# Norm work in single-tile pieces, statistics of four images in one group, and late sends of two images in a four-layer MetaFormer with mixtures of experts

## The reference

```python
x = x + mixer(layernorm(x))          # L0 fractal, L1 involution, L2 KAN spline, L3 attention
t = tokens(x)                        # 8192 x 128
t = t + experts(layernorm(t))        # for each token the chosen experts alone count
# layer    experts E   choices K   hidden F
#   0         8           1          512     relu, capacity 1.25, nan_to_num at the end
#   1         8           2          512     gelu, softmax over the two
#   2         8           2          256     gelu, softmax over all, top two
#   3        16           2          256     silu(x w1) * (x w2) w3, top two renormalised
def layernorm(v):
    return (v - mean(v, -1)) / sqrt(var(v, -1) + 1e-6)   # 1e-5 ahead of the experts
```

## Time and profile before

| | |
|---|---|
| runs | 2220.95, 2220.1, 2215.83 us (median 2220.1) |
| the profiled execution | 2214.52 us, its span 2212.8 us |
| mean granted TensorE clock | 0.909 |
| busy in the span | PE 1774.9, DVE 1546.8, ACT 1197.6, POOL 953.9 us |
| indirect DMAs on GpSimd | 488 returns, 448 sends |

### The profile page before, as it was taken

One profiled execution on the slowest core, in us unless ns is written; L12 is line 12 of the kernel. 1 busy time (PEld: TensorE's weight loads), 2 busy tenths in 40 slices (PEclk: granted clock), 3 DMA queues, 4 the chain that ended last, 5 costly groups with the idle time before them and its releaser, 6 DMA issues. The chain is left out here.

```text
span 2212.8 us, 44512 instructions
## 1 busy us (share of the span) xinstructions
PE 1774.9 (80%) x10980; PEld 1391.5 (63%) x10981; DVE 1546.8 (70%) x4832; ACT 1197.6 (54%) x2708; POOL 953.9 (43%) x953
## 2 busy tenths in 40 slices
PE   2588666898588888999895866797859999888986
PEld 2234566898344344899884434686657777687986
DVE  6998887689677777655776667557765777754564
ACT  4455776799233233777674333565664444454653
POOL 0000234444113443665442377777510446466664
PEclk9999766999699999999997877889969999989998
DMA  3002002232200010233341112235330002023373
GB/s 79 0 0 76 15 27 60 60 99 74 86 11 29 29 58 27 65 98 101 105 117 39 53 52 79 79 107 171 116 117 21 27 33 59 31 69 97 106 216 102
DMA packets 183598, 154.35 MB, mean 70 GB/s; under 512 B 40294, under 2 KB 162822, under 8 KB 183362
## 3 DMA queue, kind: packets, MB, share of 16 engines
q1 hardware_dynamic: 153410, 92.37, 15.6%
q0 software_dynamic: 29952, 59.26, 7.9%
HBM read 85.33 MB, written 68.79 MB: 70 GB/s over the span
## 5 line engine op out<-in xcount | busy, mean ns | idle before, releaser
L1706 POOL DMA_INDIRECT returned<-rows_second_choice x488 | 506.9, 1039 | 370.7 <-DVE rows_second_choice L1631 151.7
L1492 PE MATMUL psum<-rows_first_choice 128*128 128x128 f32 x2816 | 387.3, 282 | 28.7 <-DVE rows_first_choice L1612 27.8
L1263 POOL DMA_INDIRECT dispatched<-rows_first_choice,slot x192 | 191.5, 998 | 487.1 <-DVE rows_second_choice L1159 434.9
L1492 PEld LDWEIGHTS psum<-rows_first_choice 128*128 128x128 f32 x2816 | 352.0, 196 | 38.0 <-DVE rows_first_choice L1612 36.7
L1502 PE MATMUL psum<-expert_weights,rows_first_choice 128*128 x2240 | 325.4, 284 | 28.3 <-DVE rows_second_choice L1628 11.8
L1502 PEld LDWEIGHTS psum<-expert_weights,rows_first_choice 128*128 128x128 f32 x2240 | 284.4, 195 | 41.7 <-issue 37.4
L1562 ACT ACTIVATE rows_first_choice<-psum,bias_columns 128x128 f32<-128x128 f32 x832 | 238.7, 374 | 106.9 <-PE psum L1492 105.3
L1263 POOL DMA_INDIRECT dispatched<-rows_second_choice,slot x192 | 187.6, 977 | 58.5 <-issue 58.2
L1263 POOL DMA_INDIRECT dispatched<-rows_first_choice,expert_weights x64 | 62.0, 969 | 267.2 <-DVE rows_first_choice L1157 249.9
L1545 ACT ACTIVATE rows_first_choice<-expert_weights 128x512 f32 x216 | 137.3, 636 | 40.2 <-issue 40.1
L1484 PE MATMUL psum<-identity,rows_second_choice 128*128 128x128 f32 x488 | 138.4, 285 | 16.2 <-DMA rows_second_choice<-dispatched 16.1
(11 more groups left out here) (416 smaller groups left out, 3814.3 us busy)
## 6 DMA issues: line engine op xcount, KB each, us to landing
rows_second_choice<-dispatched SPq DMA_DIRECT2D x488, 65.0 KB
rows_second_choice<-returned SPq DMA_DIRECT2D x10, 1024.0 KB, 5.5
returned<-rows_second_choice POOLq DMA_INDIRECT x488
expert_weights<-in_L_ffn_w SPq DMA_DIRECT2D x3, 2048.0 KB, 8.6
expert_weights<-returned SPq DMA_DIRECT2D x6, 1024.0 KB, 5.4
channel_major<-returned SPq DMA_DIRECT2D x6, 1024.0 KB, 5.7
residual<-in_x SPq DMA_DIRECT2D x8, 512.0 KB, 7.3
rows_second_choice<-returned SPq DMA_DIRECT2D x8, 512.0 KB, 4.0
```

Source lines behind the costliest of these rows:

```text
L1263: pool.indirect_dma_start(out=self.k.dispatched, out_offset=bass.IndirectOffsetOnAxis(ap=self.slot[:, b % 2, c, t:t + 1], axis=0), in_=sel ...
L1492: ins = pe.matmul(k.ps[:, self.PSH + u % 2, j * P:(j + 1) * P], self.wc[:, u % 2, j * P:(j + 1) * P], self.xt[:, u % 2, :], start=True, st ...
L1706: pool.indirect_dma_start(out=k.returned[0:N * self.K, :], out_offset=bass.IndirectOffsetOnAxis(ap=self.rt[:, u, C:C + 1].bitcast(I32), ax ...
```

## The change

- **Opening**: `norm.vector` stands ahead of the wait for GpSimd and of the four casts.
- **NormStage**: statistics in groups of four, two and two images in place of four pairs. A table STEPS for each layer, with one small piece a tile: an add of half an image (128x512), four bn_stats, one Newton round, two or three norms. Images 6 and 7 are both done after the last tile in every layer.
- **GpSimd**: in layer 0's tail it adds six images to x (128x1024). In layer 1's tail it adds the two choices of six images into each other in the room they were loaded to, and VectorE adds that to x in halves. In layer 2's tail VectorE adds both choices in halves.
- **LastStage**: later loads and stores, adds in halves at other steps.
- **Last layer**: five first images (64 first tiles in place of 48). Images 6 and 7 are sent between the returns: image 6 one block every second tile from tile 0, image 7 one every fourth tile from tile 16. In layer 1 image 7's blocks go every second tile.
- VectorE reads the next tile's expert number ahead of the norm piece in layers 1 and 2.

```diff
@@ opening
             ins.then_inc(s_set.h, 1)
-            dve.wait_ge(s_set.h, 7)
+            norm.vector(dve)
             dve.wait_ge(s_made.h, 8)
             dve.tensor_copy(k.rank[:], int_rank[:])
...
-            norm.vector(dve)
@@ class NormStage
-    PAIRS = B // 2
+    GROUPS = ((0, 1, 2, 3), (4, 5), (6, 7))
-    LOAD_AFTER = [None, (55, 56, 60, 64, 68, 71), (87, 91, 99, 107, 115, 123), (88, 92, 104, 110, 118, 124)]
-    PAIR_AT = [None, (46, 54, 62), (78, 94, 110), (92, 108, 124)]
-    SIXTH_AT = [None, None, 126, None]
-    TAKE = [None, (0, 2), (0, 3), (0, 3)]
-    FINISH = [None, 4, 6, 6]
-    INVERT = [None, 6, 9, 9]
+    STEPS = [
+        None,
+        dict(load=(55, 56, 60, 64, 68, 71), fold=(43, 44, 48, 52, 56, 60), collect=(50, 52, 54, 58, 63, 67),
+             finish=(60, 69), root=(61, 70), offset=(62, 71), norm=(63, 65, 67, 69, 72, 74),
+             turn=(65, 67, 69, 71, 74, 76), keep=(66, 68, 70, 72, 75, 77)),
+        dict(load=(87, 88, 89, 93, 103, 119), fold=(75, 77, 79, 83, 91, 107), add=(80, 84, 88, 92, 105, 112),
+             collect=(82, 86, 90, 94, 107, 114), finish=(96, 116), root=(97, 117), offset=(101, 121),
+             norm=(102, 104, 106, 108, 122, 124), turn=(105, 107, 109, 111, 125, 127),
...
+        dict(load=(87, 88, 89, 97, 103, 119), add=(78, 84, 90, 96, 116, 122), collect=(82, 88, 94, 100, 120, 126),
+             finish=(102, 128), root=(103, 129), offset=(107, 133), norm=(108, 110, 112, 114, 134, 136),
...
+    def gpsimd_step(self, pool, t):
+
+        for b in range(B - 2):
+            if self.adds < 4 and t == self.steps["fold"][b]:
+                pool.wait_ge(self.s_back[b].h, self.s_back[b].base + 16)
+                xs, room = self.image(b), self.room(b)
+                if self.choices == 1:
+                    pool.tensor_tensor(xs, xs, room, ALU.add).then_inc(self.s["rows_added"].h, 1)
+                else:
+                    pool.tensor_tensor(room[:, :, 0:C], room[:, :, 0:C], room[:, :, C:2 * C],
+                                       ALU.add).then_inc(self.s["choices_folded"].h, 1)
...
+    def add_folded(self, dve, b, h):
+
+        dve.wait_ge(*self.when("choices_folded", b + 1))
+        xs = self.image(b)[:, self.half(h)]
+        dve.tensor_tensor(xs, xs, self.room(b)[:, self.half(h), 0:C], ALU.add).then_inc(self.s["rows_added"].h, 1)
...
+    def add_half(self, dve, b, c, h):
+
         if c == 0:
             dve.wait_ge(self.s_back[b].h, self.s_back[b].base + 16)
...
-    LEFT = 24
+    LEFT = 12
@@ class LastStage
-    LOAD_AFTER = (96, 98, 100, 102, 112, 128)
+    LOAD_AFTER = (112, 114, 116, 118, 120, 128)
     COMPLETE = 128
-    ADD_AT = (88, 91, 94, 97, 104, 120, 136)
-    STORE_AFTER = (108, 111, 114, 117, 124, 140)
+    ADD_AT = (104, 108, 112, 116, 120, 126, 138)
+    STORE_AFTER = (122, 126, 130, 134, 138, 142)
@@ Router, TAILS
-FIRST_IMAGES = 4
+FIRST_IMAGES = (4, 4, 4, 5)
+HELD_FROM = (7, 7, 7, 6)
...
-        for b in range(B - 1):
+        for b in range(HELD_FROM[self.layer]):
             self.send(pool, b)
...
-    dict(pe=(0, 4, 5, 8), dve=(0, 2, 6, 9, 10), act=(2, 4, 7), send=9),
-    dict(pe=(0, 6, 8, 12), dve=(0, 3, 9, 13, 14), act=(3, 6, 10), send=12),
-    dict(pe=(0, 6, 8, 12), dve=(0, 3, 9, 13, 14), act=(3, 6, 10), send=12),
...
+    dict(pe=(0, 4, 5, 8), dve=(0, 2, 6, 9, 10), act=(2, 4, 7), send={7: (9, 2)}),
+    dict(pe=(0, 6, 8, 12), dve=(0, 3, 9, 13, 14), act=(3, 6, 10), send={7: (12, 1)}),
+    dict(pe=(0, 6, 8, 12), dve=(0, 3, 9, 13, 14), act=(3, 6, 10), send={6: (0, 2), 7: (16, 4)}),
@@ class Experts
             if at >= self.table_end:
+                if self.vector_copies and t + 2 < self.T:
+                    ahead.append(self.expert_of(dve, t + 2))
                 self.following.vector_step(dve, t)
...
+            for b, (start, every) in held.items():
+                if t == start:
+                    route.slots_known(pool, b)
+                    pool.wait_ge(*route.sent(b - 1, b % 2))
+                n = t - start
+                if 0 <= n < TPB * every and n % every == 0:
+                    route.send_tile(pool, b, n // every)
...
+            if t >= self.table_end:
+                self.following.gpsimd_step(pool, t)
```

More of the change, by code:

```diff
@@ L459, in gpsimd, with image, half @@
             self.involution.make_gather(pool)
-    def add(self, dve, b, c):
-        k = self.k
+    def image(self, b):
+        return self.k.x[:, b * TPB:(b + 1) * TPB, :]
+    @staticmethod
+    def half(h):
+        return slice(h * TPB // 2, (h + 1) * TPB // 2)
+    def add_folded(self, dve, b, h):
[3 more added lines that the diff above has]
+    def add_half(self, dve, b, c, h):
         if c == 0:
@@ L526, in invert, with norm @@
         self.offset(dve, g, 1)
-    def norm(self, dve, b, by_scalar):
+    def norm(self, dve, b, js, last):
         k = self.k
@@ L590, in vector @@
         for b in (B - 2, B - 1):
-            if b == B - 1 or not self.SIXTH_AT[self.layer]:
-                for c in range(self.choices):
-                    self.add(dve, b, c)
-                self.collect(dve, b)
-        g = self.PAIRS - 1
+            self.add_late(dve, b)
+            self.collect(dve, b, 0)
+            self.collect(dve, b, 1)
+        g = len(self.GROUPS) - 1
         self.finish(dve, g)
@@ L598, in vector @@
         for b in (B - 2, B - 1):
-            self.norm(dve, b, self.BY_SCALAR_LATE[self.layer])
+            self.norm(dve, b, [j for j in range(TPB) if j not in self.BY_SCALAR_LATE[self.layer]], True)
         if self.spline:
@@ L767, in scalar, with add @@
         pass
-    def add(self, dve, b, c):
+    def add(self, dve, b, c, h):
+        half = slice(h * TPB // 2, (h + 1) * TPB // 2)
         if c == 0:
```

226 lines of the change are left out of this document (120 added, 106 removed).

## The result

The changed kernel takes 2165.9 us (median of 4 runs, 2162.91 to 2169.21) where the kernel before, run beside it, takes 2218.0; the ratio is 0.9769 (95% interval 0.9742 to 0.9797). Forecast were 2179, between 2155 and 2204. The profiled execution took 2167.17 us, its span is 2165.3 against 2212.8.

What follows compares the result with a forecast made beforehand. The prediction saw 140 us in which TensorE waits between tiles. Its terms, -8.1 + 5 - 11.5 - 3 - 11.7 - 11, made -40: 2174.5 us against the profiled execution, about 2179 by medians, 2155 to 2204 holding 8 in 10.

Steps and rivals of the forecast that it cites:

- Opening, -8.1: Start of the kernel: VectorE's first bn_stats starts at 5.1 us instead of 13.24, and nothing later hides it; bounds -9.2 and -7.5.
- Layer 0, +5: Layer 0's tail: VectorE's relief -3, GpSimd's code load +6, images 4 and 5 normed after the last tile +2; ends -4, +12.
- so of 7.3 us I count less than half, -3: Layer 0's tail: VectorE gives up six adds of 1.22 us, but ScalarE and TensorE are nearly full, so only -3.
- Layer 1, -11.5: Layer 1's tail: smaller pieces leave 14 of 27.4 us excess, gaining 13.4; image 6 after the last tile costs 1.9.
- Layer 2, -3: Layer 2's tail: smaller pieces gain, VectorE's new wait for the first image's rows costs 11, earlier end -2; ends -14, +8.
- take about 12 of the 34 us: Layer 2's tail: half adds, single Newton rounds and pairs of norms win about 12 of the 34 us that can be won.
- Layer 3, -22.7: Last layer: -11.7 in the first stretch from sends between returns, -11 in the second from half adds and later loads.
- it is the bound: Layer 3's first stretch: GpSimd's 77 operations in 109 us, 99 us of 1.28, set the pace.
- All of it hides: Rival, chance 0.20: code load falls in GpSimd's idle time, layers 0 to 3 give -4, -17, -8, -24; -61, about 2158.
- GpSimd stays the bound of layer 3's start: Rival, chance 0.15: tile 64 starts as before, second stretch gains 7, the rest holds; -25, about 2194.
- about no change: Rival, chance 0.06: full code load, folds blocking VectorE, full landing wait, layer 3 -8, opening -8; 0, about 2219.
- Slower: Rival, chance 0.04: GpSimd's code must be loaded at every switch between add and indirect DMA; +26, about 2246.

## Why the prediction came out as it did

**Opening, -8.1 (measured -8.9): right number, and half of the cause.** The step "behind the casts, which wait for GpSimd's counting columns" described the kernel before well, and the edit is enough by itself (first tile at 361.5 with the gap back: -8.1 on the dot). But the prediction took GpSimd's gap of 9.3 us as fixed. It depends on what the execution ahead called last, and the change removes it too, so in the changed kernel the edit adds only 0.5 us (360.7 against 361.2).

**Layer 0, +5 (measured +12.9): the failed step is "so of 7.3 us I count less than half, -3".** It counted the adds on GpSimd as free but for the first call. The call cost 4.3 us (6 forecast) and the part behind the last tile, with two more norms in it, is 2.6 longer (2 forecast; the kernels of before differ by 1.8 there). But under four of the six adds an operation of VectorE takes 2.3 to 2.8 us more than usual, under the other two VectorE waits for the add, and with the lower granted clock behind the waits the adds cost 8.1. The finer steps alone gave -2.4 (73.8 against 76.2). The prediction priced just this effect in layer 1 (4 us) and forgot it here, where VectorE was busy 56.6 of 61 us. The Trainium skill (GPSIMD Engine Reference, Elementwise) had spoken against the move, and here it was right: neither use of GpSimd for adds paid.

**Layer 1, -11.5 (measured -16.1).** The tail went from 131.9 to 117.0 us, -14.9, where the text had -13.4; behind the last tile, where image 6 is now added, it is 2.3 longer (1.9 forecast), but that part varies by 4.6 between the kernels that have it. The rest, -3.5, lies ahead of tile 80, behind image 7's sends, for which nothing was in the sum; it is between -1.7 and -3.5 in the runs with the same edit. No run undid those sends alone.

**Layer 2, -3 (measured -13.5): the failed step is "take about 12 of the 34 us".** The wait was well read (10.8 us; tiles 72 to 88 are 13.1 longer). Between tiles 88 and 135 the smaller pieces brought 24.9, not 12. Nor is that the wait coming back: with 3.7 us of wait in place of 10.8 the same tiles take 72.2 us, not more than 1.7 above the changed kernel. TensorE is busy 62.8 and VectorE 62.5 of the 70.5 us there; had the sum gone by TensorE's 72.4 busy us of before, out of 96, it would have given 23.6.

**Layer 3, -22.7 (measured -21.9): the second half right, the first right by luck.** Undoing the sends costs 12.6 us in the first half, so they are what gained it. But -11.7 was the middle between 0 and -21 (worked out exactly it is -10.6), and the path of the sum was wrong: it put the bound on GpSimd's 77 operations ("it is the bound") and let tile 64 start once the return of tile 44 and the table are through. GpSimd held the loads only up to tile 35; the return of tile 45 already waited 3.8 us for VectorE. What stood in the way of tile 48 was SyncE's queue, with a pad behind each load (2.2 us a tile), the table and then the load, a term that the sum doesn't have. After the change tile 64 starts 15 tiles of 1.5 us behind tile 49, as TensorE runs freely, and not behind the table. In kernels with the new sends tile 64 stands at 119.5 to 122.6 us, so that the difference of 0.1 from the forecast says nothing. The second half came for the reasons given: the half add fits VectorE's idle time and finds its rows. The loads there are 16, 16, 16, 16, 8 and 0 tiles later, not "10 to 16".

**The rivals.** "All of it hides" had layers 1 and 3 about right (-17 and -24) and layer 0 wrong by 17 us. "GpSimd stays the bound of layer 3's start" and "about no change" didn't happen. "Slower" didn't either: there is one gap ahead of the first add and none later. The range held in part by luck, since the errors of layers 0 and 2, 7.9 and 10.5 us, have opposite signs.

On GpSimd and VectorE at the same memory: beside a whole add a return takes 1.54 us, and in layer 1's tail here one takes 1.48 beside a half add, which the Trainium skill (SBUF — State Buffer, Who interferes with whom) excludes for a tensor_tensor; the other direction, an exclusive hold for the whole instruction, is as the page says: 0.29 us became 2.56, 0.68 became 2.54. The prediction counted halves and whole adds as the same to the returns. In the last stage they aren't: in its last 80 tiles ten returns took more than 1.3 us before and none after, and beside its half adds a return takes about 1.15.

## What to carry to other kernels

Where work is spread finely between the tiles, the stretch ended near the busy time of its busiest engine, so forecast it from that time and not from a share of the excess. Here that engine was busy 89 to 99% of the spread tails of layers 1 to 3, and 85% in layer 0 with GpSimd's adds in it. Helping VectorE with a two-input add on GpSimd saved it nothing, since copies, two-input adds and tensor_scalar operations of VectorE waited for the whole of the other's 2.35 us. Look also at the queue that issues the loads: a second small DMA behind each load held the last layer at 2.2 us a tile where TensorE could do 1.5, and no engine's busy time shows that. And where GpSimd's last call of a program is for other code than its first, one tiny call at the end can move a gap of 9 us out of the start of the next execution.

## What was not expected of the hardware

- The gap of GpSimd's first select is 9.3 us (10.4 in the kernel without GpSimd's adds) or 0, by what the program, and so the previous execution, called last: the all-reduce or an add; first calls of an add had 6.9, 7.3 and 8.4 us of idle ahead.
- Waits of a few us in layer 0's tail brought the granted clock from 1.00 to 0.87 and 0.92 in the windows around them, worth 6.6 us of TensorE's busy time.
- Of three loads of 1 MB issued within 3.5 us the second took 8.5 us, and beside them three tiles waited 1.3 to 2.3 us for their 65 KB loads; beside a single one, in the kernel before, a tile waited 2.7.
- Loads of a tile left SyncE's queue 1.1 us apart at the least, and with a pad write behind each 2.2.
- While GpSimd adds, VectorE's bn_stats of one tile (0.28 us) run as ever.
